# The gathered rows of a graph layer added on VectorE instead of TensorE, with fewer blocks of sums

## The reference

```
h = relu(layernorm(x))
e = concatenate([h[src], h[dst]], axis=1)            # 200000 x 128
m = relu(e @ W1 + b1) @ W2 + b2                      # hidden 128, output 64
s = segment_sum(m, dst);  cnt = segment_sum(1, dst)  # per node
return x + s / maximum(cnt, 1)[:, None]
```

## Time and profile before

| | |
|---|---|
| median of 3 runs | 2846.46 us (2843.46 to 2848.26) |
| the profiled execution | 2839.25 us, of which the span of its instructions is 2837.4 us |
| busy PE / DVE / ACT / POOL | 1548.3 / 1428.9 / 1189.8 / 1372.7 us |
| mean granted TensorE clock | 0.749 of full speed |

### The profile page before, as it was taken

How to read it: one execution, slowest core, us unless ns; L and a number is a source line. 1 busy time by engine, 2 the same in 40 slices (tenths; PEclk the granted TensorE clock), 3 DMA queues, 4 the chain that set the end, 5 groups by cost and what they waited for, 6 DMA issues and landing times.

```text
span 2837.4 us, 26976 instructions
## 1 busy us (share of the span) xinstructions
PE 1548.3 (55%) x8249; PEld 1183.2 (42%) x8250; DVE 1428.9 (50%) x3051; ACT 1189.8 (42%) x2414; POOL 1372.7 (48%) x1460
## 2 busy tenths in 40 slices
PE   1656565566465564455544555455455545555556
PEld 0545353444344443344433444344344434434444
DVE  3554343343324665456655666456565556655421
ACT  1223343444314544345444454344344444444444
POOL 6345545445555445444554435545544554554553
PEclk6878777788787777677776777767776777776778
DMA  4532222222134656556565566556565665665541
GB/s 90 163 109 60 59 61 59 60 59 58 58 98 144 202 181 189 167 169 200 179 192 154 178 188 200 186 159 183 184 192 168 186 191 174 183 186 157 174 119 43
DMA packets 258990, 408.46 MB, mean 144 GB/s; under 512 B 45128, under 2 KB 118749, under 8 KB 258841
## 3 DMA queue, kind: packets, MB, share of 16 engines
q1 hardware_dynamic: 211845, 312.84, 35.7%
q0 software_dynamic: 46432, 93.61, 12.5%
q10 hardware_dynamic: 564, 0.23, 0.0%
HBM read 388.12 MB, written 18.38 MB: 143 GB/s over the span
## 4 chain that ended last, share of the span: by engine, by line
PE 48%; issue 36%; another core or an unknown queue 9%; DVE 6%; ACT 1%; DMA 0%; DVEq 0%; SPq 0%; ACTq 0%
PE z L1374 16%; PE bank L1401 12%; PE z L1386 10%; DVE g L1153 4%; PE bank L1419 2%; PE bank L1408 2%; PE z L1445 2%; PE bank L1430 1%; PE z L1461 1%; DVE rows_b L936 1%; PE bank L1268 1%; DVE norms L920 1%; PE z L1268 1%; ACT g L812 0%
## 5 line engine op out<-in xcount | busy, mean ns | idle before, releaser
L672 POOL DMA_INDIRECT g<-p_table,src_e x1403 | 1326.1, 945 | 1425.3 <-PE bank L1401 960.5
L1153 DVE SCALAR_TENSOR_TENSOR g<-z,norms,g 128x1024 bf16<-128x1024 f32 (+1 forms) x884 | 1019.1, 1214 | 43.5 <-issue 25.3
L812 ACT ACTIVATE g<-z 128x1024 f32<-128x1024 f32 x182 | 185.6, 1020 | 1468.0 <-remote 1153.5
L1100 DVE TENSOR_TENSOR acc<-acc,bank 65x128 f32 x191 | 54.2, 284 | 1201.0 <-remote 1069.7
L1374 PE MATMUL z<-work 128*128 128x128 f32 x1464 | 258.8, 348 | 514.2 <-issue 482.9
L1374 PE MATMUL z<-w,work 128*128 128x128 f32 x1438 | 251.9, 345 | 484.3 <-issue 443.8
L1374 PEld LDWEIGHTS z<-work 128*128 128x128 f32 x1464 | 240.3, 256 | 546.0 <-issue 541.7
L1374 PEld LDWEIGHTS z<-w,work 128*128 128x128 f32 x1438 | 234.4, 253 | 512.3 <-issue 509.3
L1401 PE MATMUL bank<-work,g 128*128 128x128 f32 x2902 | 423.4, 307 | 15.4 <-issue 15.1
L1401 PEld LDWEIGHTS bank<-work,g 128*128 128x128 f32 x2902 | 414.1, 227 | 16.8 <-issue 16.7
L1386 PE MATMUL z<-g,ident 128*128 128x512 f32 x726 | 350.8, 605 | 5.8 <-issue 5.7
(11 more groups left out here) (161 smaller groups left out, 1063.6 us busy)
## 6 DMA issues: line engine op xcount, KB each, us to landing
g<-tally_table SPq DMA_DIRECT2D x816, 256.0 KB
rel_q<-rel_table SPq DMA_DIRECT2D x46, 512.0 KB
rows_b<-rel_table SPq DMA_DIRECT2D x45, 512.0 KB
g<-p_table,src_e POOLq DMA_INDIRECT x1403
g<-tally_table SPq DMA_DIRECT2D x68, 128.0 KB
work<-q_table SPq DMA_DIRECT2D x96, 64.0 KB
w<-q_table SPq DMA_DIRECT2D x96, 64.0 KB
g<-p_table SPq DMA_DIRECT2D x12, 512.0 KB
```

Of the source, the lines that this page charges most:

```text
L672: nc.gpsimd.indirect_dma_start(out=g[:, slot(n), j * HID:(j + 1) * HID], out_offset=None, in_=p_table, in_offset=bass.IndirectOffsetOnAxis ...
L812: nc.scalar.activation(rows_of_p(m), z[:, 0:HID * chunks_in(m)], ACT.Relu).then_inc(r_done, 1)
L1153: nc.vector.scalar_tensor_tensor(product[i % BUFFERS][:, 0:w], turned[:, 0:w], minus_q[:, d:d + 1], tally_row[i % BUFFERS][:, 0:w], ALU.ma ...
```

## The change

`add_rows` goes from TensorE to VectorE: one `tensor_tensor` that reads `z` (PSUM) and the gathered rows (`g`) and writes over the latter, after `spread_q` of that couple. `relu` then works in place in `g`, so `z` is free again once VectorE has read it, and `spread_q(m + 1)` waits for `z_done` in place of `r_done`. TensorE's program for a round becomes

```diff
-Q0 = 28
+Q0 = 26
-GROUP_SIZES = ((128, 4), (320, 2), (QT * 128, 1))
+GROUP_SIZES = ((126, 4), (320, 2), (QT * 128, 1))
+def wide(blocks):
+    joined = []
+    for groups_k in blocks[:-2]:
+        if joined and period(joined[-1][0]) == period(groups_k[0]) and len(joined[-1]) + len(groups_k) <= MOST_GROUPS:
+            joined[-1] = joined[-1] + groups_k
+        else:
+            joined.append(groups_k)
+    return joined + blocks[-2:]
+MOST_GROUPS = 4
+BLOCKS = wide(BLOCKS)
-ROUND_TALLIES, TALLY_ROUND, TALLY_PLACES = 6, 3, 12
-VECTOR_TALLIES = (1, 4)
+ROUND_TALLIES, TALLY_ROUND, TALLY_PLACES = 5, 3, 10
...
             def relu(m):
                 act.wait_ge(z_done, m + 1)
-                nc.scalar.activation(rows_of_p(m), z[:, 0:HID * chunks_in(m)], ACT.Relu).then_inc(r_done, 1)
+                nc.scalar.activation(rows_of_p(m), rows_of_p(m), ACT.Relu).then_inc(r_done, 1)
...
+            def add_rows(m):
+                dve.wait_ge(zq_done, m + 1)
+                if 2 * m < RAW:
+                    dve.wait_ge(raw_p_done, 2 * m + 2)
+                else:
+                    dve.wait_ge(gathered[slot(Q0 + 2 * m) // 2], rows_landed(m))
+                nc.vector.tensor_tensor(rows_of_p(m), z[:, 0:HID * chunks_in(m)], rows_of_p(m), ALU.add)\
+                    .then_inc(z_done, 1)
...
                         for p in tallies(m):
                             high_hot_of(p)
+                        add_rows(m)
                         dense(m)
...
                 pe.wait_ge(spread_done, parts_to(m + 1))
                 if m:
-                    pe.wait_ge(r_done, m)
+                    pe.wait_ge(z_done, m)
...
-            def add_rows(m):
-
-                if 2 * m < RAW:
-                    pe.wait_ge(raw_p_done, 2 * m + 2)
-                else:
-                    pe.wait_ge(gathered[slot(Q0 + 2 * m) // 2], rows_landed(m))
-                for n in couple(m):
-                    w = HID * chunks_of(n)
-                    last = nc.tensor.matmul(z[:, 512 * (n % 2):512 * (n % 2) + w], ident[:, :], g[:, slot(n), 0:w],
-                                            start=False, stop=True)
-                last.then_inc(z_done, 1)
...
-                for m in range(COUPLES):
-                    add_rows(m)
-                    if m >= 2 and m - 2 == BLOCK_END[BLOCK[m - 2]]:
+                for m in range(COUPLES + 3):
+                    if m - 1 in (COUPLES - 2, COUPLES - 1):
+                        sum_edges(m - 1)
+                    if 2 <= m < COUPLES + 2 and m - 2 == BLOCK_END[BLOCK[m - 2]]:
                         times_w2(BLOCK[m - 2])
-                    dense(m)
+                    if 1 <= m < COUPLES - 1:
+                        sum_edges(m - 1)
                     if m + 1 < COUPLES:
                         spread_q(m + 1)
-                    sum_edges(m)
+                    dense(m)
```

More of the change, by code:

```diff
@@ L81, with period @@
         BLOCKS.append([i])
+def period(i):
+    return (GROUPS[i][0] - Q0) // 8
+def wide(blocks):
[8 more added lines that the diff above has]
+BLOCKS = wide(BLOCKS)
 BLOCK = [k for m in range(COUPLES) for k, groups_k in enumerate(BLOCKS) if GROUP[Q0 + 2 * m] in groups_k]
@@ L170 @@
 MEMBER_FROM = PRODUCT_ROUND
-def on_vector(p):
-    return p % ROUND_TALLIES in VECTOR_TALLIES
-def on_scalar_to(p):
-    return sum(not on_vector(k) for k in range(p))
 def products_in(m):
@@ L304, in gnn_kernel @@
         low_hot = [above_ring(512 + 256 * k, 256, BF16) for k in range(TALLY_PLACES)]
-        high_hot = [above_ring(3584 + 64 * k, 64, BF16)[:, 0:125] for k in range(TALLY_PLACES)]
-        tally_stage = above_ring(4352, 256, U16)[0:125, :]
-        q_dense = above_ring(4352, 128, F32)[0:DENSE, :]
+        high_hot = [above_ring(3072 + 64 * k, 64, BF16)[:, 0:125] for k in range(TALLY_PLACES)]
+        tally_stage = above_ring(3712, 256, U16)[0:125, :]
+        q_dense = above_ring(3712, 128, F32)[0:DENSE, :]
         tally_row = [above_ring(512 * k, 512, U16) for k in range(BUFFERS)]
@@ L313, in gnn_kernel @@
         digit_i, digit, src_of_edge = (norms[:, NC * k:NC * (k + 1)] for k in range(3))
-        high_key, low_key = (norms[:, NC * k:NC * (k + 1)] for k in (3, 4))
-        minus_q, added = (norms[:, SPANS * DENSE + DENSE * k:SPANS * DENSE + DENSE * (k + 1)] for k in range(2))
-        by_count, low_seen = minus_q, norms[:, 1086:1086 + TALLY_PLACES]
-        edges_d, of_node = norms[0:125, 1060:1060 + DGROUPS], norms[0:125, 1080:1080 + PER_GROUP]
-        assert 5 * NC <= SPANS * DENSE and (SPANS + 2) * DENSE <= 1060 and DENSE <= NC and DGROUPS <= 20 and TALLY_PLACES <= 14
+        high_key, low_key = (norms[:, SPANS * DENSE + NC * k:SPANS * DENSE + NC * (k + 1)] for k in range(2))
+        added, by_count = (norms[:, SPANS * DENSE + DENSE * k:SPANS * DENSE + DENSE * (k + 1)] for k in range(2))
+        minus_q = norms[:, 1020:1020 + DENSE]
+        edges_d, of_node = norms[0:125, 1081:1081 + DGROUPS], norms[0:125, 1095:1095 + PER_GROUP]
+        assert 3 * NC <= SPANS * DENSE and SPANS * DENSE + 2 * NC <= 1020 and DENSE <= min(61, NC) and DGROUPS <= 14
         work = sb("work", [128, STAGES * UNIT_COLS + 512])
@@ L409, in edges_of, with sums_of @@
             return table[:, t, :].rearrange("q (c e) -> q c e", c=4)
+        def sums_of(k):
+            return sums_u[:, 2 * WIN:] if k == len(BLOCKS) - 1 else sums_u
         def chunks_of(n):
@@ L846, in dense @@
                         stage_tallies(i)
-                of = [p for p in tallies(m) if not on_vector(p)]
+                of = tallies(m)
                 for p in of[0:1]:
                     far_low_of(p)
-                for p, after in zip(of, of[1:] + [None]):
-                    if after:
-                        far_low_of(after)
+                for p in of:
+                    if p + 1 in of:
+                        far_low_of(p + 1)
                     low_hot_of(p)
@@ L1418, in times_w2 @@
                 pe.wait_ge(u_copied, k + 1)
-                nc.tensor.matmul(v_of(k)[0:FEAT, 0:w], w2[:, :], sums_u[:, k % 2, 0:w],
+                nc.tensor.matmul(v_of(k)[0:FEAT, 0:w], w2[:, :], sums_of(k)[:, 0:w],
                                  start=True, stop=True).then_inc(v_psum, 1)
@@ L1437, in tally @@
                 pe.wait_ge(high_hot_done, p + 1)
-                if not on_vector(p):
-                    pe.wait_ge(low_hot_done, on_scalar_to(p + 1))
+                pe.wait_ge(low_hot_done, p + 1)
                 if p == TALLY_FIRST[i]:
@@ L1536, in window_general @@
                     pe.wait_ge(u_moved, m)
-                    nc.tensor.matmul(v_bank[0:FEAT, 0:WIN], w2[:, :], sums_u[:, 0, 0:WIN],
+                    nc.tensor.matmul(v_bank[0:FEAT, 0:WIN], w2[:, :], sums_u[:, 0:WIN],
                                      start=True, stop=True).then_inc(v_made, 1)
```

51 lines of the change are left out of this document (18 added, 33 removed).

## The result

The changed kernel takes **2545.63 us** (median of 4 runs, 2539.78 to 2560.13), the kernel before 2844.96 us on the same chip (4 runs). The ratio is **0.895, 95% interval 0.891 to 0.900**: 299 us faster. The profiled execution is 2549.84 us with a span of 2548.0, 289.4 us less than before.

A forecast was written before the change was run, and what follows sets the result against it. TensorE was taken to get little visible done from 5 us into each gather batch until 3.1 us past it. 2837.4 - 215 - 59 + 48 + 14 = 2625 us of span, 2634 us as median; range 2290 to 2890 us.

The forecast's parts named there:

- The addition: add_rows moved from TensorE to VectorE: 1.22 us each there; 1.88 us of matmuls leaving TensorE save nothing by themselves.
- Free batches: Gather batches whose next couple is all queued before the batch ends: 19.66 + 3.15 + 0.26 = 23.1 us.
- Held batches: Gather batches after which addition, spread_q and sum_edges all follow the release: 19.66 + 3.15 + 8.2 = 31.0 us.
- Tallies and blocks: Five wide tallies a round on ScalarE and 100 products with W2 fewer on TensorE: counted as nothing.
- Rounds with tallies: 22 gather batches beside tallies: 26 us each in place of 28.7, together -59 us.
- Starts of spans: Twelve turns of a new span by TensorE, the addition behind waiting products: +48 us, ends 0 and 96.
- 26 quads: Quads by counts: eight gathers more, half a batch, +14 us; 117 products fewer on VectorE give nothing.
- the likeliest case: Free and held batches alternating in rounds with products: 2634 us, range 2500 to 2760 us, chance 0.45.
- the stretch with products: Batches in rounds with products: mean 27.0 us in place of 30.7 by alternation, 58 x 3.7 = -215 us.
- theory A: In the experiments: the gain is in what TensorE has queued during a batch, decided by sum_edges one round later.
- all held: Rival: spread_q always ends later than 5 us into the batch, each batch 0.3 us longer; 2932 us, chance 0.18.
- The hold isn't there without `add_rows` on TensorE: Rival: GpSimd then issues gathers without a pause; some 2000 us, chance 0.04.

The follow-up runs named there:

- run 7: Changed kernel with each gathered row 32 columns wide in place of 128 from the second turn of the ring on: 2501.98 us, ratio 0.884.
- run 8: Changed kernel with one gather for each quad in place of four from the second turn of the ring on: 1778.17 us, ratio 0.628.
- run 6: Kernel before with only the addition on VectorE, relu in place and spread_q waiting for z_done: 2520.5 us, ratio 0.891.
- run 2: Changed kernel with blocks not joined, of one or two groups as before: 2582.83 us, ratio 0.912.
- run 5: Changed kernel with the product with W2 behind sum_edges in place of ahead of it: 2481.67 us, ratio 0.876.
- run 1: Changed kernel with TensorE's old order, the addition still on VectorE and blocks still joined: 2463.93 us, ratio 0.872.
- run 4: Kernel before with only the blocks joined, 100 products with W2 fewer: 2770.4 us, ratio 0.978.
- run 9: Kernel of run 1 with GpSimd waiting before each two quads for one couple, on the third chip: 1855.97 us, ratio 1.006.
- run 10: Changed kernel with every product over half its span of sources, on the third chip: 1860.93 us, ratio 1.008.
- run 12: Kernel of run 1 with AHEAD_LEAST 26 in place of 8, gathers running as far ahead to the end, third chip: 1858.85 us, ratio 1.007.

## Why the prediction came out as it did

*The reading of what bounds the kernel* was right in the main for the chip of the main comparison: most signals of TensorE come late from some 5 us into a batch until 3.1 us past it, and the period is made of that. In the earlier trace rows the 16 rows don't go one by one, as the prediction reads them, but in ones, twos and threes, and the addition of 1297.16 shows a signal in mid-batch. Runs 7 and 8 show that it isn't the bytes of the gathers, and that four gathers in a row aren't enough. What the prediction didn't see is that this is not a property of the kernel alone: on the third chip of the experiments the same instructions have no such effect.

*The addition.* Taken as 1.22 us, measured 1216 ns. That it saves nothing by itself, and that the gain is in what can be queued, was the right place to look; run 6 shows that the move to VectorE with `z` freed early is enough for the whole gain, without the new order.

*Free batches.* 23.1 us forecast, 23.18 measured, with GpSimd's idle time at 3.47 (3.4 forecast). The five of the stretch from 1210 take 23.2 to 24.2.

*Held batches.* This is the step that failed: "the next batch needs the addition 1.22, `spread_q(x + 3)` 3.75, `sum_edges(x + 2)` 2.95", 31.0 us in all, behind a `spread_q` that "starts 5.8 us in and is held". In the batch of 1233.29 `spread_q` starts 0.93 us in (1234.22), because ScalarE had made its one-hots in the batch before (1222.62); by the prediction's own condition that batch should be free. In the batch of 1283.62 it does start late, 5.0 us in, and isn't held to the release. In both, the prediction's "If they come only then" fails.

The couple whose sum the next batch waits for had its addition inside the held batch (1241.26 and 1297.16). At the first batch's release its `sum_edges` stands in TensorE's queue with all it needs, and only its 3.39 us are left. From the last gather's end, 3.12 us to the release (1256.11), 0.36 to its start, 3.39, and 0.27 until the gather starts are 7.1 us of idle time, and a batch of 26.84 us. The prediction had a held batch held one step earlier than it is. What stands ahead of that `sum_edges` in TensorE's queue, and can account for its lateness, is this: the first `sum_edges` of the batch waited for a copy and a product with `W2` (1235.11 to 1240.4), `spread_q` came after it (1242.58), and then the transposing matmuls of the means (L1432) went through in the slow stretch.

From 1210 to 1465 the batches alternate, as forecast, but between 23.2 to 24.2 us and 26.8 to 28.0, with idle times of 3.5 to 4.5 and 7.2 to 8.3 us, not 3.4 and 11.3. Elsewhere the turns are less clean, with batches of 25 to 26.5 us between them: of the 61 batches behind the tally rounds only 15 last under 24.6 us, a quarter and not half.

*Batches at the end.* Not foreseen: from 2073 us on a batch takes 28.7 us, since a product with `W2` comes in each of them and stands ahead of `sum_edges`. "Tallies and blocks" were put at nothing; in the changed kernel the joining is worth some -45 us (run 2), and the product's place ahead of `sum_edges` some +54 (1.9 points, run 5), both with 15 us of uncertainty.

*Rounds with tallies.* 26 us forecast. Without the one long interval in that stretch, 38.8 us (44.3 before), they are (604.4 - 38.8) / 22 = 25.7, and the term is -66 us in place of -59.

*Starts of spans.* Put at +48 us, measured as nothing that shows: from 1210 to 1465, over two starts, the idle times keep their alternation, and TensorE's transposes for them (L1462) waited 0.7 us for VectorE in all.

*26 quads.* +14 us forecast; run 1 beside runs 4 and 6 puts quads, tallies and products together at 0 within some 12 us, if the parts multiply.

*The sum.* 2634 us forecast, 2545.63 measured: inside the range of the likeliest case, with its gain put 88 us too low. That it isn't farther off is partly luck, since fewer batches are free than forecast and the held ones are shorter. For the parts: -215 + 48 = -167 us for the stretch with products, measured -233.7. Held batches some 3.5 us shorter than forecast explain the larger gain where free and held ones alternate; the slow batches at the end took part of it back. The new order of TensorE's program, which the section on the change describes as "`sum_edges` stands one round later" and on which theory A was built, gives nothing beside the addition on VectorE: it costs 2.3 points.

*The rival "all held"* failed on the same step as the forecast of the held batch. *"The hold isn't there without `add_rows` on TensorE"* is refuted on the chip of the main comparison by 475.5 us of late signals at the addition. On the third chip the times are 1847 to 1861 us (the kernel before and runs 9, 10 and 12), for another reason than the rival's.

A rule of the Trainium skill bears on the hold: "SBUF — State Buffer", section "Who interferes with whom", says that TensorE and ScalarE never wait on anyone there. The third chip's rows fit it. The rows of the other chips don't, if the hold is at SBUF at all, which no run here can say; there the measurement decides.

## What to carry to other kernels

When an engine's signals come late in a stretch that recurs, ask what must be in its queue before the stretch begins, and free the buffer that gates it (here `z`, by an addition of 1.2 us on another engine); keep behind it everything that itself waits for one of the late signals, such as a product that needs a copy. Here two things were moved at once, and the runs don't tell which of them is needed. Compare orders by the sequence that the engine sees, not by the round in which the code writes it: a step "one round later" can be no move at all. And before a kernel is tuned around such a stretch, time it on other chips: here the best version by these measurements (run 1, 2464 us, 0.872 of before, with run 5's 0.876 next to it) lives with something that one of the three chips of the experiments did not show.

## What the runs showed of the hardware

- In the main comparison and on the first two chips of the experiments, TensorE's matmul rows go through singly or in twos and threes while GpSimd issues indirect DMAs back to back: 16 rows over 14 us in the earlier trace rows, with 1.82 and 1.73 us idle before a row in run 6. It ends about 3 us after the last one (3.08 and 3.12 us in the changed kernel). A signal can still come through in between, 13.5 us into the batch of 1283.62. On a third chip, with the same gathers at the same pace, that is absent in the profiles of four kernels, and the kernel before takes 1847 us in place of 2831. Whether that is the chip or the occasion (all runs of a chip stand within minutes of each other), and what differs, stays open.
- A quarter of the bytes for each row leaves both the issuing time (946 ns) and the hold as they are. Four gathers in a row hold nothing; sixteen do.
- A `tensor_tensor` of VectorE over 128 x 1024 f32 with one operand in PSUM, written back over the other, takes 1216 ns on the chip with the hold and 1217 ns on the one without it (run 12), beside gathers on both.
